# Local attention layers of a one-core kernel: one 384-column projection per tile, values carried by DMA, three steps per pair of heads

## What is computed

```python
def local_attention(q, k, v):            # windows of 32, each looks at itself and the one before
    mask = (it < jb) | (it > jb + w) | (jb == -1)
    sim = jnp.einsum('bhwie,bhwje->bhwij', bq, bk2) * QK_SCALE
    attn = jax.nn.softmax(jnp.where(mask, -big, sim), -1)
    return jnp.einsum('bhwij,bhwje->bhwie', attn, bv2)
...
def attn_layer(x, Wqkv, qs, ksc, Wo):    # 16 heads of 64
    q, k, v = split(x @ Wqkv)
    q = l2norm(q) * qs; k = l2norm(k) * ksc
    q = q * cos * scale + rotate_half(q) * sin * scale
    k = k * cos / scale + rotate_half(k) * sin / scale
    return local_attention(q, k, v) @ Wo
...
for i in range(6):
    x = attn_layer(shift_tokens(x), ...) + x
    x = ffn_layer(shift_tokens(x), ...) + x    # LayerNorm, W1, gate by Gelu, W2
```

## Time and profile before

| what | value |
|---|---|
| runs | 5904.95, 5897.06, 5900.51 us; median 5900.51 |
| span of the profiled execution, first to last instruction | 5900.4 us |
| instructions | 159891 |
| PE busy | 5495.2 us (93%), 60258 matmuls |
| PEld busy | 3949.3 us (67%) |
| DVE busy | 4294.8 us (73%) |
| ACT busy | 4093.6 us (69%) |
| POOL busy | 2762.7 us (47%) |
| mean granted clock of PE | 0.965 |
| DMA queue of SP | 128056 packets, 76.74 MB, 4.6% of 16 engines' span |

### The profile page before, as it was taken

How to read it: one execution, slowest core, us unless ns; L and a number is a source line. 1 busy time by engine, 2 the same in 40 slices (tenths; PEclk the granted TensorE clock), 3 DMA queues, 4 the chain that set the end, 5 groups by cost and what they waited for, 6 DMA issues and landing times. The chain is left out here.

```text
span 5900.4 us, 159891 instructions
## 1 busy us (share of the span) xinstructions
PE 5495.2 (93%) x60258; PEld 3949.3 (67%) x60258; DVE 4294.8 (73%) x6692; ACT 4093.6 (69%) x7768; POOL 2762.7 (47%) x2483
## 2 busy tenths in 40 slices
PE   8998986899999999999998899899999999999998
PEld 3334443678777777777776333677777778777776
DVE  7876654777777777777775886777777777777775
ACT  5774654677777777777775577677777777777775
POOL 1101100566655665556663110566556666556663
PEclk8997998899999999999999899999999999999999
DMA  0000000100000000000000000100000000000000
GB/s 13 2 2 6 2 3 8 36 17 16 19 14 19 17 16 20 15 18 16 16 21 10 4 2 2 36 17 16 20 13 19 17 16 21 16 17 16 17 20 18
DMA packets 128857, 87.46 MB, mean 15 GB/s; under 512 B 33332, under 2 KB 121936, under 8 KB 128056
## 3 DMA queue, kind: packets, MB, share of 16 engines
q1 hardware_dynamic: 128056, 76.74, 4.6%
HBM read 68.96 MB, written 1.05 MB: 12 GB/s over the span
## 5 line engine op out<-in xcount | busy, mean ns | idle before, releaser
L1733 POOL TENSOR_TENSOR cross<-raw,tab_b 128x512 f32<-128x512 f32 x768 | 998.1, 1324 | 304.6 <-ACT raw L1600 301.8
L737 DVE TENSOR_REDUCE arena<-PS 128x1 f32<-128x512 f32 (+3 forms) x1408 | 828.4, 646 | 216.4 <-PE PS L550 130.5
L1739 POOL CAST kT_b<-kT 128x512 bf16<-128x512 f32 x384 | 311.9, 812 | 1318.2 <-ACT kT L1656 1318.2
L688 ACT ACTIVATE arena<-PS 128x1024 f32<-128x1024 f32 (+1 forms) x704 | 668.4, 968 | 203.1 <-PE PS L573 126.3
L1853 DVE TENSOR_TENSOR oT<-PS,rec_den 128x288 f32<-128x288 f32 (+1 forms) x768 | 326.2, 425 | 635.2 <-ACT rec_den L1634 635.2
L1824 DVE TENSOR_TENSOR rot<-PS,tab_a 128x512 f32<-128x512 f32 x768 | 521.9, 686 | 227.9 <-PE PS L1451 133.8
L1406 PE MATMUL PS<-qT,kT 64*128 64x96 f32 x8448 | 660.6, 287 | 0.0
L1626 ACT ACTIVATE PT<-PS 128x576 f32<-128x576 f32 (+1 forms) x768 | 468.7, 610 | 257.9 <-PE PS L1406 245.3
L1600 ACT COPY raw<-PS 128x512 f32<-128x512 f32 x768 | 447.1, 589 | 285.5 <-PE PS L1451 244.8
L1840 DVE TENSOR_TENSOR rot<-rot,cross 128x1024 f32<-128x1024 f32 x384 | 613.4, 1597 | 17.8 <-POOL cross L1733 17.4
L1847 DVE TENSOR_TENSOR rot<-rot,inv_norm 128x1024 f32<-128x1024 f32 x384 | 578.6, 1507 | 10.6
(11 more groups left out here) (260 smaller groups left out, 13084.0 us busy)
## 6 DMA issues: line engine op xcount, KB each, us to landing
w_qk<-in_w_pairs SPq DMA_DIRECT2D x196, 128.0 KB, 2.1
w_v<-in_w_pairs SPq DMA_DIRECT2D x100, 128.0 KB, 2.2
w_o<-in_w_out_pairs SPq DMA_DIRECT2D x192, 64.0 KB, 1.9
xs<-staged SPq DMA_DIRECT2D x24, 224.0 KB, 2.6
w<-in_L_ffn_W SPq DMA_DIRECT2D x12, 341.0 KB
q_parts<-max_rows SPq DMA_DIRECT2D x192, 2.0 KB
V<-in_c_E SPq DMA_DIRECT2D x2, 896.0 KB, 8.3
w<-in_L_ffn_W SPq DMA_DIRECT2D x24, 64.0 KB
```

What stands on the lines that cost most here:

```text
L688: nc.scalar.activation(PT[u % 6].rearrange("p (a n) -> p a n", a=2)[:, :, first_q:512], PS[:, 2 * (u % 2):2 * (u % 2) + 2, first_q:512], A ...
L737: nc.vector.tensor_reduce(maxima[:, 2 * m + h, qt, kh:kh + 1], bank[:, 0:keys_of(qt, kh)], AX.X, ALU.max).then_inc(bank_free, 1)
L1733: nc.gpsimd.tensor_tensor(dst[:, :, :, o:o + 32], src[:, :, :, other:other + 32], tab[:, :, o:o + 32].unsqueeze(2).broadcast_to([128, 8, 2 ...
```

## The change

- `query_keys` and the V fills become `projections`: for each 128-token tile three products of 384 columns (queries, keys and values of one pair together), one bank a tile, Q0 to Q7. Two neighbouring banks are read together: one `raw_copy` of 128 x 2 x 384 into a `raw` that is now 384 wide, one `by_cosine` of 2 x 256, which releases both (`filled_pair`, `release_of`; releases are counted instead of taken as number / 4).
- The overlapping value chunks are put together by DMA: `gather_values`, seven transfers from `raw` to `V` per pair, issued by SP when all four raw copies of the pair are done. Together they move 1344 pieces of 512 bytes. The next pair's first raw copy waits for them (`values_in`), the first `values` of the pair too. `V` holds one pair, in two buffers. Its edges are set to zero once.
- `STEPS` becomes chunks 0-3, 4-7, 8-10; PT, log_den and rec_den are wider.
- Order: `maximum(1)` stays at its place, `maximum(0)` is done at the end of the pair that projects it, after K1 and q1 (for the following pair's attention). Q6 and Q7 (`projections(3)`) and both output halves stand between scores 0 and scores 1. Between `max_rows` and scores 0 nothing stands. ACT and DVE follow.
- One weight tile of 384 columns per pair, one split of it on POOL.

```diff
-        STEPS = ((0, (0, 1, 2)), (0, (3, 4)), (1, (5, 6, 7)), (1, (8, 9, 10)))
+        STEPS = (range(0, 4), range(4, 8), range(8, 11))
+        NS = len(STEPS)
...
-                values_of = {0: {0: [0], 5: [1], 1: [2, 3], 3: [4, 5]}, 7: {}}.get(p, {5: [0], 3: [1]} if p % 2 else {0: [2], 5: [3], 1: [4], 3: [5]})
...
-            names = (["Q0", "Q1"] if a else []) + (["x0", "x1", "x2", "x3"] if bb else []) + (["Q2", "Q3"] if a else [])
+            names = (["Q0", "Q1", "Q2", "Q3"] if a else []) + (["x2", "x3"] if bb else []) + (["Q4", "Q5", "Q6", "Q7"] if a else [])
...
+            def filled_pair(eng, l, b, p, i):
+
+                need(eng, full, fill(l, b, p, f"Q{2 * i + 1}") + 1)
+                bank = bank_of(l, b, p, f"Q{2 * i}")
+                return PS[:, bank:bank + 2, 0:384], free[bank]
...
+                def gather_values(p):
+
+                    for r, key, rows, tile, at, first, n in ((0, 0, 32, -1, 96, 1, 2), (0, 32, 96, 0, 0, 0, 3), (1, 0, 64, 0, 64, 0, 3), (1, 64, 64, 1, 0, 0, 3),
+                                                             (2, 0, 96, 1, 32, 0, 3), (2, 96, 32, 2, 0, 0, 2), (3, 0, 128, 2, 0, 0, 2)):
+                        c, t = 4 * first + r, 3 * first + tile
+                        sp.dma_start(V[p % 2][key:key + rows, c:c + 4 * n - 3:4, :], raw[at:at + rows, t:t + 3 * n - 2:3, 256:384]).then_inc(values_in, 16)
...
+                        need_apart(sp, pv_full, it * NS - NS)
+                        need_apart(sp, raw_in, it * 4 + 4)
+                        gather_values(p)
+                        need_apart(sp, wqkv_split, it * 2 + 4)
...
+                    for t in range(2 * i, 2 * i + 2):
+                        bank = bank_for(l, b, p, f"Q{t}")
                         for n, (m, w) in enumerate(PRODUCTS):
-                            last = nc.tensor.matmul(bank[:, 256 * j:256 * j + 256], x_parts[b][m][:, PAD + 128 * t:PAD + 128 * t + 128], wqk_parts[w][:, :],
+                            last = nc.tensor.matmul(bank[:, 0:384], x_parts[b][m][:, PAD + 128 * t:PAD + 128 * t + 128], wqkv_parts[w][:, :],
                                                     start=n == 0, stop=n == 2)
...
                     if a:
-                        query_keys(l, b, p, 0)
-                        query_keys(l, b, p, 1)
+                        projections(l, b, p, 0)
+                        projections(l, b, p, 1)
                     if oo:
-                        values(r - 1, 3, (p + 6) % 8)
+                        values(r - 1, NS - 1, (p + 6) % 8)
                     if bb:
-                        maximum(l, b, p, 0)
                         maximum(l, b, p, 1)
                     if a:
-                        query_keys(l, b, p, 2)
-                        query_keys(l, b, p, 3)
-                    late(l, b, p, 0)
+                        projections(l, b, p, 2)
                     if bb:
                         max_rows(l, b, p)
-                    late(l, b, p, 5)
-                    if bb:
                         scores(l, b, p, r, 0)
+                    if a:
+                        projections(l, b, p, 3)
                     late(l, b, p, 1)
...
+                    late(l, b, p, 4)
+                    if a:
...
+                        maximum(l, b, p, 0)
...
                     need(act, cross_done, item(l, b, p) * 4 + (2 * (i // 2) - 2))
-                    bank, _ = filled(act, l, b, p, f"Q{i}")
-                    nc.scalar.copy(raw[:, 2 * i:2 * i + 2, :].rearrange("p t n -> p (t n)"), bank).then_inc(raw_in, 1)
+                    if i == 0:
+                        need(act, values_in, item(l, b, p) * GATHERS)
+                    banks, _ = filled_pair(act, l, b, p, i)
+                    nc.scalar.copy(raw[:, 2 * i:2 * i + 2, :], banks).then_inc(raw_in, 1)
...
                         square(l, b, p, 0)
                         raw_copy(l, b, p, 2)
-                        raw_copy(l, b, p, 3)
-                    late(l, b, p, 0)
                     if bb:
                         rows_in(r)
-                    late(l, b, p, 5)
+                        exps(r, 0)
                     if a:
                         inverse_norm(l, b, p, 0)
-                    if bb:
-                        exps(r, 0)
-                    if a:
+                        raw_copy(l, b, p, 3)
                         square(l, b, p, 1)
```

More of the change, by code:

```diff
@@ new lines, in bank_of, with leader, releases, releases_before @@
+        def bank_of(l, b, p, name):
+            return (names_at(l)[1] + place(l, b, p, name)) % 4
+        def leader(names, n):
+            return n - (names[n][2] in ("Q1", "Q3", "Q5", "Q7"))
+        def releases(names, base, bank):
+            return [n for n in range(len(names)) if leader(names, n) == n and (base + n) % 4 == bank]
+        def releases_before(l, bank):
+            in_first, in_layer = len(releases(FIRST, 0, bank)), len(releases(LAYER, N0, bank))
+            if isinstance(l, int):
+                return 0 if l == 0 else in_first + in_layer * (DEPTH - 1)
+            return l * in_layer + (in_first - in_layer)
@@ L1754, in position @@
                         cross_terms(l, b, p, 1)
[L1755 to L1756 removed]
+                        need(pool, full, fill(l, b, p, "Q7") + 1)
+                        split_weights(it + 1)
                     if ff and p == 1:
@@ L1937, in position @@
                         normalise(l, b, p, 1)
-                    for s in range(1, 4):
+                    for s in range(1, NS):
                         late(l, b, p, s + 1)
-                        if bb and s < 3:
+                        if bb and s < NS - 1:
                             quotients(r, s, (p + 1) % 2)
+                    late(l, b, p, 4)
+                    if a:
+                        maxima(l, b, p, 0)
                 def bring_in(b):
```

273 lines of the change are left out of this document (129 added, 144 removed).

## The result

| | kernel before | changed kernel |
|---|---|---|
| time, median (range) | 5901.0 us (5897.1 to 5905.0) | 6393.1 us (6383.3 to 6395.0) |
| ratio | | 1.083, 95% interval 1.081 to 1.084 |
| span | 5900.4 us | 6381.5 us |
| PE busy | 5495.2 us | 5447.6 us |
| mean granted clock of PE | 0.965 | 0.939 |

The account below looks back on a forecast made before the run. PE's instruction stream was taken as the bound. Work saved and waits added, pair by pair, came to +80 us in 22 batches and +17 in the two without feed-forward: 5900.5 + 97 = 5997 us, range 5790 to 6130.

Parts of the forecast that it names:

- PE's work: Matmuls and steps over a batch's eight pairs: PE does 8.75 us less, 210 us in 24 batches.
- Wait 1: PE idle before the first scores of every pair, waiting for ACT's rows R: 1.15 us.
- Waits 2 and 3: PE waits for DVE's normalised first and second K and q: 0.7 and 0.9 us in even pairs, second 1.0 in odd.
- The transfers: Seven gathers per pair after raw copy 3, landing at 19.4 us, hidden by 1.4 us at the least.
- Rival 2: Gathers land late and hold ACT's raw copy in 96 even pairs: 211 us, 6208 in all; chance 0.07.
- The faster one: Rival that the work won outweighs the waits: 5827 us, or 5690 with no wait left; chance 0.26.
- The turning point: Added waiting in a pair below which the change wins: 1.1 us, from 8.75/8.
- The third: Rival that 384-column matmuls cost what 512 do: projections rise by 276 us, to 6273; chance 0.03.

Follow-up runs that it names:

- e1: Changed kernel with SP starting the seven value gathers before anything else in each slot; 6185.5 us (ratio 1.048).
- e3: On top of e1, ACT copies the row maxima R before the raw copy of projections 4 and 5; 6144.1 us (ratio 1.042).
- e2: Changed kernel without the seven value gathers and the waits for them, V left at zero; 6192.3 us in one run.
- e7: On top of e3, ACT's feed-forward rstd moved behind the copies of K1 and q1, and X1 one slot earlier in pair 7; 6047.0 us (ratio 1.024).
- e4: On top of e1, the projected tiles taken in four steps again instead of three; 6286.2 us (ratio 1.065).
- e12: On top of e7, DVE normalises the first half early or adds sines before quotients, chosen pair by pair; 5989.8 us (ratio 1.015).
- e6: On top of e1, projections 6 and 7 put between row maxima and first scores on PE, ACT reordered; 6322.1 us (ratio 1.072).

## Why the prediction was wrong, step by step

**PE's work: right in kind, a fifth too much.** The 384-column products start 0.176 us apart (0.178 taken): ten steps from 2000.38 to 2002.14. By the earlier trace rows and e1's stretches PE's busy time falls by 2.84, 0.37, 1.54, 0, 1.35, 0.37 and 1.33 in pairs 0 to 6 and rises by 1.0 in the last, together 6.8 us a batch for the 8.75 put. In 24 batches that is 163 for 210 us, 47 of the miss.

**Wait 1: there in all 192 pairs, 0.9 for 1.15.** Shown by e3, since R moved ahead halves it. Priced too high, by 47 us. But e3 also shows that a wait isn't worth its own sum: 94 us of it went and the time fell by 41.

**Waits 2 and 3: the right place, in even pairs too small.** The even pair of the changed kernel without feed-forward, first, then the odd one:

```profile
PE PS L1535 <- DVE rot L1868: 2.2, 2, 1.5
...
PE PS L1535 <- DVE rot L1868: 0.8, 1, 0.8
```

0.8 and 1.5 for the 0.7 and 0.9 that I had put, and 0.8 for 1.0 in the odd one. The periods alternate, at 20.25 and 22.22 where 19.4 and 22.5 were forecast. Of the 0.85 that the even pair ran over, the three waits together make 0.4 (3.2 for 2.75); the other 0.4 is PE's work, 17.06 where the forecast leaves 16.65. Among the waits, what ran over (first projection at 1096.54) is the second half on DVE, in its timeline:

```profile
1111.36 1.66 DVE L1861 TENSOR_TENSOR rot<-rot,cross 128x1024 f32<-128x1024 f32 x1
1113.05 1.91 DVE L1868 TENSOR_TENSOR rot<-rot,inv_norm 128x1024 f32<-128x1024 f32 x1
```

I had taken the normalisation at its mean, 1.51; the one that matters takes 1.91. Over the whole changed kernel the mean of the normalisation is 1.69, and that of the sine 1.29, where 1.60 was put.

**The transfers: the failed step.** The prediction put "Queued behind them on SP are only the weights for two pairs on" and so found the gathers "hidden, by 1.4 us at the least". I asked what stands behind them and not what stands ahead. Their size was priced well enough: seven issues take 4.65 us (6.0 put), and they land in 2.2 to 2.5 (2.6 put). What failed is the start. In 22 pairs, in which SP has more to do, the gathers are issued 9 to 14 us after `raw` is full. In 72 of the other 170 pairs, odd ones all, they are 3.3 to 4.0 us late as well, behind the loads of `w_o`; but in all 170 they land 2 us or more before the next raw copy, so there they are hidden as predicted. e1 prices the 22 at 208 us. Rival 2 had the right end, ACT's raw copy held by the gathers, by another mechanism (landing too slow, in all even pairs); by chance its 211 us are close to the 208. The Trainium skill's warning on small transfers (DMA: Bandwidth & Descriptors, measured bandwidth) fits the landing times, 2.2 us for 32 KB and 2.5 for 144 KB, nearly all of it fixed. But it did not bite: e2 shows all seven free once they start in time.

**Pairs 2, 3 and 7: once-per-batch work that I had not followed.** ACT's `rstd` ahead of the copy of K, and the bank of X1, 38 and 40 us of waits; e7 gets 97 back. Before, the rstd came when its moments had long been there: the fourth step stood in between. e4, which puts that step back, shows it. ACT's waits for the moments, in the kernel before, the changed one and e4:

```profile
ACT rstd L1640 <- DVE moments L1875: 27.6, 2, 14.6
ACT rstd L1679 <- DVE moments L1896: 94.6, 24, 16.0
ACT rstd L1679 <- DVE moments L1895: 26.2, 2, 13.1
```

The 22 waits are gone in e4, and so are the two rows of PE. I had looked for cover of the steps that the pairs share and taken the feed-forward's pieces as given.

**The clock: in no term.** The changed kernel has 1.2 GHz for 787 us, the kernel before for 415; of the 372 more, 315 lie in pairs 2, 3 and 7 and 44 in pairs 0. What stood behind a long wait was reckoned at full clock.

**The sum.** From 5997: the gathers' order 208, the two moves 97, PE's work 47; that is 6349 of 6393. The 44 left are wait 1 too high (minus 47) against even pairs too low and the turn of the hardware loop, where PE's first projection waits 31 us in 8 turns in e1 for 17 in the kernel before. These were read off, not tested, and the 97 was measured on top of e3 and not on the changed kernel, so that the terms need not add up exactly.

**The rivals.** The faster one, at 0.26, is refuted even in the best form: in e12 waits 2 and 3 are still 153 us. The turning point was 1.1 us of added waiting per pair (0.85 by the measured work); in e1 idle time grew from 7.0 to 25.3 us a batch, 2.3 per pair. The third (384 columns cost like 512) fell with 0.176.

**Three readings.** The DMA share in the earlier trace rows is 2 to 10 hundredths and not 3 to 12; POOL is busy for 61% of those eight stretches and not about half; and by the prediction's own list four pairs, not three, lose at least 1.7 us of PE's work. None of them moves a term of the sum.

## What to carry to other kernels

A transfer that takes over a computing engine's work inherits the order of the queue that issues it: go through every position of that queue in which something stands ahead of it, the rare ones above all, and ask what those wait for. When a step is cut from a pipelined loop, list what it covered not only for the loop's own chain but for each piece that is hung into it once per round. And add waits on TensorE with the clock: in the batch above 7.5 us of idle time brought 6.2 us of slow work behind them.

## What I had not expected of the hardware

The price of a long wait on PE was more than the wait. In the changed kernel's pair 2, cut at the wait:

```profile
2067.33:2070.85 3.52, 3.52 (x36) 2.75 (x28) 1.06 (x2) 0.11 (x1) 0.95 (x2) 1.00 0.08 13
2070.85:2079.06 8.21, 0.00 (x0) 0.03 (x1) 0.83 (x2) 1.76 (x3) 0.10 (x1) 0.72 0.50 118
2079.06:2091.54 12.48, 11.53 (x88) 9.06 (x88) 6.68 (x9) 6.03 (x11) 4.04 (x4) 0.50 0.02 5
2091.54:2101.82 10.28, 6.83 (x98) 4.94 (x97) 9.19 (x24) 6.29 (x15) 6.68 (x5) 1.00 0.34 83
```

An idle 8.2 us is followed by 12.5 us at clock 0.50, that is 1.2 GHz, though PE is busy for 11.5 of them. The projections start 0.32 us apart there instead of 0.176. In e6 an idle 2.98 us was followed by it, while the four waits of 0.85 to 1.70 us in e1's pair 2 of this batch leave the clock at 1.00. Such waits are not always free: in 4 of e1's 22 such pairs, with none over 1.86, the clock fell to 1.2 GHz early in pair 3. The Trainium skill (TensorE: Matmul & The Clock Gate, HAM oscillation) warns of gaps between matmuls for this reason; the rows of the long waits agree.

An issue on SP takes time of its own: 0.63 us for a gather, in all 4.65 us a pair for seven, in which SP does nothing else. The Trainium skill (DMA: Bandwidth & Descriptors, its table of where the fixed time goes) calls the making of descriptors small and says that many can be emitted before it shows. The trace agrees in so far as gathers of 64 and of 288 pieces both take 0.63 us (medians). What held up the gathers here is the number of issues: eight rows of scales, at 0.35 to 0.38 us each (medians) and with what stands between them, took 5 us.
